# One value block of an attention kernel is made at step 5 and none at step 22

## The reference

```python
xn = _layernorm(x, axis=-1)
q = einsum('bse,hde->bhsd', xn, Wq) + bq      # 16 heads of 64; k and v alike
scores = where(causal, -inf, einsum('bhsd,bhtd->bhst', q, k) / scale)
att = softmax(scores, axis=-1) / scale
z = einsum('bhst,bhtd->bhsd', att, v)
x = x + z.reshape(b, s, h * dh) @ proj + ffn(xn)
```

## Time and profile before

| | us |
|---|---|
| median of 3 runs | 1348.27 |
| lowest and highest of them | 1347.8, 1348.32 |
| the profiled execution | 1347.42 |
| its span, first to last instruction | 1345.7 |

### The profile page before, as it was taken

One profiled execution on the slowest core, in us unless ns is written; L12 is line 12 of the kernel. 1 busy time (PEld: TensorE's weight loads), 2 busy tenths in 40 slices (PEclk: granted clock), 3 DMA queues, 4 the chain that ended last, 5 costly groups with the idle time before them and its releaser, 6 DMA issues.

```text
span 1345.7 us, 34453 instructions
## 1 busy us (share of the span) xinstructions
PE 1330.3 (99%) x10783; PEld 1131.7 (84%) x10783; DVE 1106.3 (82%) x4001; ACT 1085.9 (81%) x3162; POOL 997.7 (74%) x1443
## 2 busy tenths in 40 slices
PE   7999999999999999999999999999999999999998
PEld 5788888888888888888888888888888888888887
DVE  8978888788787878878788787888878888788785
ACT  6887887888788887887888788788888887888785
POOL 7887777778777777777777768777677876778664
PEclk9999999999999999999999999999999999999999
DMA  6455444544544445454444544454454454545541
GB/s 155 95 119 118 103 112 113 122 104 111 125 107 116 105 113 123 103 122 110 116 103 115 123 103 115 112 122 110 103 124 113 103 122 112 122 95 119 118 103 48
DMA packets 112561, 150.59 MB, mean 112 GB/s; under 512 B 18239, under 2 KB 47230, under 8 KB 112382
## 3 DMA queue, kind: packets, MB, share of 16 engines
q1 hardware_dynamic: 111086, 147.97, 46.8%
q10 hardware_dynamic: 1296, 0.42, 0.2%
HBM read 10.69 MB, written 4.19 MB: 11 GB/s over the span
## 4 chain that ended last, share of the span: by engine, by line
PE 95%; ACT 1%; SPq 0%; POOL 0%; DVE 0%; DMA 0%; issue 0%; DVEq 0%; POOLq 0%
PE zp L1323 22%; PE ptp L1297 20%; PE jobp L1167 13%; PE scores L1285 9%; PE scores L1288 7%; PE outp L1335 7%; PE jobp L1172 6%; PE scores L1266 4%; PE scores L1263 3%; PE jobp L1182 1%; PE outp L1344 1%; PE jobp L1187 1%; PE jobp L1360 0%; PE jobp L1177 0%; ACT prob L721 0%; PE outp L1349 0%
## 5 line engine op out<-in xcount | busy, mean ns | idle before, releaser
L632 POOL TENSOR_TENSOR prob<-prob,rden 128x128 f32<-128x128 f32 (+3 forms) x1024 | 712.4, 720 | 247.2 <-DVE rden L971 240.7
L982 DVE CUSTOM_DVE_ANT_0 prob<-scores,mask 128x128 f32<-128x128 f32 (+3 forms) x1024 | 471.7, 488 | 199.8 <-issue 133.3
L721 ACT ACTIVATE prob<-prob,nmax 128x128 f32<-128x128 f32 (+3 forms) x1024 | 567.5, 559 | 12.1 <-DVE nmax L982 5.4
L1297 PE MATMUL ptp<-ident,prob 128*128 128x128 f32 x2560 | 366.9, 274 | 2.1 <-ACT pt L732 1.5
L1297 PEld LDWEIGHTS ptp<-ident,prob 128*128 128x128 f32 x2560 | 295.0, 140 | 27.4 <-POOL prob L632 5.0
L1323 PE MATMUL zp<-pt,v_sb 128*64 128x64 f32 (+3 forms) x4096 | 307.7, 303 | 0.0
L732 ACT ACTIVATE pt<-ptp 128x128 f32<-128x128 f32 (+3 forms) x512 | 221.2, 432 | 102.8 <-PE ptp L1297 102.8
L1323 PEld LDWEIGHTS zp<-pt,v_sb 128*64 128x64 f32 x4096 | 221.6, 137 | 51.2 <-issue 19.7
L994 DVE COPY pt<-ptp 128x128 f32<-128x128 f32 (+3 forms) x512 | 243.3, 475 | 3.9 <-PE ptp L1297 3.1
L571 POOL CAST k_low<-k_lo 64x512 fp32r<-64x512 f32 x256 | 156.0, 609 | 78.0 <-DVE k_lo L866 68.1
L1285 PE MATMUL scores<-k_twice,q_parts 128*128 128x384 f32 (+1 forms) x512 | 200.9, 392 | 0.0
(11 more groups left out here) (192 smaller groups left out, 2003.3 us busy)
## 6 DMA issues: line engine op xcount, KB each, us to landing
k_twice<-k_hi SPq DMA_DIRECT2D x506, 128.0 KB, 2.3
q_parts<-q_lo SPq DMA_DIRECT2D x256, 128.0 KB, 2.4
q_parts<-q_hi SPq DMA_DIRECT2D x254, 128.0 KB, 2.3
xin<-in_L_attn_x_dram SPq DMA_DIRECT2D x16, 256.0 KB, 3.1
xres<-in_L_attn_x_dram SPq DMA_DIRECT2D x16, 256.0 KB, 3.1
out_dram<-osb SPq DMA_DIRECT2D x15, 256.0 KB, 2.6
pt<-in_L_attn_Wq_dram SPq DMA_DIRECT2D x1, 512.0 KB, 4.8
pt<-in_L_attn_Wk_dram SPq DMA_DIRECT2D x1, 512.0 KB, 5.6
```

Of the source, the lines that this page charges most:

```text
L632: nc.gpsimd.tensor_tensor(part, part, scale, ALU.mult).then_inc(pn_ready, 1)
L721: nc.scalar.activation(part, part, ACT.Exp, bias=nmax[:, s % NROT, h:h + 1], scale=-1.0, accum_out=den[:, s % NROT, h:h + 1]).then_inc(p_r ...
L982: nc.vector.tensor_tensor_reduce(out=prob[:, s % NROT, h, 0:cols], in0=scores[bank][:, first_col:first_col + cols], in1=mask[:, S - cols:S ...
L1297: done = nc.tensor.transpose(ptp[h][:, P * j:P * j + P], prob[:, s % NROT, h, P * j:P * j + P], ident[:])
```

## The change

Seven of eight value blocks keep a step of the old list, but the fourth (n = 3) is made at step 5, which had no job, n = 4 to 7 move one place up to steps 6, 10, 14 and 18, and step 22 has no job. In batch 0 TensorE waits before the first block of the second half of the heads for the low parts of the weights that it needs (`w_lo_ready` 6); before, the first such block stood at step 10, behind the same wait in `values` at step 9.

```diff
-V_STEPS = (29, 30, 2, 6, 10, 14, 18, 22)
+V_STEPS = (29, 30, 2, 5, 6, 10, 14, 18)
@@ step of TensorE
                 if unit is not None:
                     transpose(c, unit)
+                if first and s == V_STEPS[NBLK]:
+                    pe.wait_ge(w_lo_ready, 6)
                 if not tail and s in JOBS and not (last and s in AHEAD):
                     job(c, s)
```

## The result

The changed kernel takes 1351.36 us (median of 12 runs, 1349.52 to 1352.13), the kernel before 1348.13 us beside it (12 runs, 1347.45 to 1348.4). The ratio is 1.0025, with a 95% interval of 1.0017 to 1.0033: slower by 3.2 us, where 1.0 us had been forecast, and 0.16 us above the end of the range. Not only the median moved: the runs now lie 2.6 us apart, before 0.95 us. The profiled execution took 1351.68 us, its span went from 1345.7 to 1349.9 us.

What follows compares the result with a forecast made beforehand. TensorE, a stream without holes in batches 1 to 15, was taken to bound the kernel; +0.64 + 0.75 - 0.4 = +1.0 us on the 1348.27 us median gives 1349.2 us, range 1347.5 to 1351.2 us.

Steps and rivals of the forecast that it cites:

- what comes late next: Steps 23 to 27: ScalarE and VectorE follow TensorE's earlier phase too late; 0.05 us a batch in 15 batches, +0.75 us.
- Rival B: Steps 23 to 27: late VectorE and ScalarE hold successive scores, 0.3 us a batch, 4.5 us in all, 1352.8 us; chance 0.07.
- sign of being wrong: Period falls, a gap ahead of step 5's value block, or a wait of 0.1 us or more at steps 23 to 25.
- one block for the other: Step 5 pays 0.70 us, step 22 saves 0.66 us: +0.04 us a batch, times 16, +0.64 us.
- The term for added semaphores: Values at steps 9 and 25 wait for one more satisfied semaphore: 0 taken, up to 0.03 us, 32 times, 1 us.
- step 27: Late VectorE maximum delays the second wide scores by 0.05 us a batch (0 to 0.15), 15 batches, +0.75 us.
- Batch 0: Step 5's block is absorbed at step 6, step 22's saving capped by GpSimd: -0.4 us (between 0 and -0.7).
- step 5 pays in full: The added value block at step 5 costs TensorE 0.70 us in each of 16 batches, without waiting for its bank.
- ScalarE's copy: The value copy after step 5's block, 0.58 us, falls in ScalarE's 0.95 us wait for `zp` and costs nothing.
- A: Steps 5 and 22 cancel, step 27's slack suffices, batch 0 gives all: +0 - 0.7, 1347.6 us; chance 0.25.
- C: Step 5's block finds its bank not free, 0.2 us a batch, 3.2 us: 1352.4 us; chance 0.03.
- D: TensorE's busy rows hide waiting; a more even spread gives back 0.2 us a batch or more: 1345.0 or less; chance 0.05.

Runs made afterwards that it cites:

- its control: Kernel before with the three base matmuls moved from the end of step 24 to the end of step 23: 1347.5 us.

## Why the prediction was wrong

**Wrong: what comes late next.** I asked whether the others follow TensorE when step 22 gets shorter, and answered for ScalarE, VectorE and GpSimd. The transfers of pair 6 I had dismissed a paragraph earlier, with the sentence that SyncE's transfers "have more time, and cost nothing". That holds from step 5 to step 22, and pair 6's are issued in steps 21 and 22 and used at step 24, across the free step. Their path runs at its own pace: key copy, four issues of 0.64 us, a landing of 2.4 us. It has 1.7 us to spare in an undisturbed batch and 0.43 us in the worst; after the change TensorE waited 2.4 us for it in the profile, and without the transfers the median is 1.7 us lower. Reading one batch only wasn't the fault here: batch 7, from which all the rows of a middle batch are, is a disturbed one, with 0.57 us to spare, less than the 0.66 us to be taken. The fault was that no row of SyncE's queue entered the working, though the earlier trace rows show a wait of 1.03 us for such a transfer in batch 0. Rival B had the place right, steps 23 to 27 and a loss of slack of 0.66 us, but the wrong carriers. Its price, 4.5 us, was too high. The prediction's own sign of being wrong, a wait of 0.1 us or more at steps 23 to 25, did appear.

**Too small: one block for the other.** +0.64 us was put, +1.5 measured. The 0.70 us of step 5 stand to 0.01 us. Of the free step I read 0.66 us off step 26, and it gives 0.59: the query job of step 23 waits for two semaphores and that of step 27 for one. With the second one moved the step behaves as step 26 does, and the period is 82.47 us beside 82.43 for its control: the +0.04 us a batch that had been put. The term for added semaphores counted 32 of them, at steps 9 and 25, but there are only 16: step 25 waits for the blocks of steps 6, 10, 14 and 18 instead of 10, 14, 18 and 22, all in one bank. At step 9 the added one costs 0.01 us or less (4.36 us in both kernels), and with step 9 filled, where step 25 does wait for both banks, step 25 takes 3.99 us as before. So the 0 taken for them holds; what costs is a second semaphore where TensorE is just coming out of a stop, and that one was there already.

**Too large: step 27.** +0.75 us was put for a maximum late at step 27. Step 27 took 2.67 us, before 2.68: nothing of it reaches TensorE. The end of my own bounds, 0, was right. VectorE's `xq_lo` does come up to 0.15 us later against step 27 in 9 of 14 batches, but the maxima behind it stand where they stood. That the time missed the range by no more than 0.16 us is luck: this term and the upper ends made room for waits that weren't in the sum.

**Batch 0.** -0.4 us was put, 0.0 measured. The block at step 5 is absorbed by step 6, as forecast. The saving at step 22 is lost at step 24, not to GpSimd but to VectorE, which in this batch forms the value bias (L962 to L965) between step 22 and 23 and comes with the maximum only then:

```profile
73.68 0.36 DVE L965 SCALAR_TENSOR_TENSOR wut<-bias_hi,late_rows,outp 32x128 fp32r<-32x128 f32 x1
74.07 0.69 DVE L982 CUSTOM_DVE_ANT_0 prob<-scores,mask 128x512 f32<-128x512 f32 x1
```

and the scores of step 24 start at 74.92 behind it, after 0.65 us of waiting:

```profile
74.92 0.36 PE L1263 MATMUL scores<-k_low,q_hi 128*128 128x256 f32 x1 [0.65 <-DVE nmax L982]
```

**Right:** TensorE sets the time, equal shapes take equal times, step 5 pays in full and waits for nothing, ScalarE's copy hides in its wait for `zp`. Rivals A, C and D fell: the steps don't cancel, the block has its bank free, and the more even spread gave nothing back: outside steps 5, 9 and 22 to 28 no step of batches 1 to 14 changed by more than 0.002 us on average.

What stays open is whether the instruction packets make the holes of some 1.3 us in SyncE's issues, or only come with them. They stand in the kernel before as well; no run took them away.

## What to carry to other kernels

Moving work on the engine that sets the time is free only if every path that runs beside the emptied place has slack for it, transfers and their issue queue included: take each consumer behind the place and ask when its last semaphore comes. Read the rows of the issuing queue as well as those of the engines, and read such slack over all repetitions, for here it is 1.7 us in half of the batches and 0.43 us in the worst, and the worst ones decide. A spread of run times that grew from 1 to 2.6 us while one step moved was here a sign of it: without the waits it went back to 1.1 to 1.3 us.

## What the hardware showed

- Four issues of 128 KB on SyncE's queue take 2.52 us, and in about half of the places looked at they or the two before them hold a hole of 1.0 to 1.4 us (3.62 to 3.95 us for four). With nearly all such holes (61 of 61 in the changed kernel's trace, 60 of 65 before) a 16 KB packet of the kind "instruction" starts within 0.3 us of the issue that is slow. TensorE's steps, where it waits for nothing, repeat to 0.01 us.
- A second semaphore, long satisfied, cost nothing where TensorE ran without a stop (in the packed trace, 0.03 us from the second transpose to the job with it and without), and 0.06 us a batch right behind a stop (82.53 against 82.47 us; 0.25 against 0.17 us from the pair of transposes to the job).
- After a stop for a transfer the first matmul of the narrow scores takes 0.11 us longer to be followed (step 24 took 2.47 instead of 2.36 us in the five batches that waited longest; in batch 6 from 571.31 to 571.53, in batch 10 from 901.64 to 901.75), on top of the stop.
